# Cross-attention of a perceiver block with 32x32 tiles: VectorE block transposes in place of TensorE transposes

## What is computed

```python
Q = split_heads(layernorm(x) @ Wq + bq)          # 16 heads of 8 channels
K = split_heads(ctx_1024 @ Wk + bk)              # ctx_1024: (128 batches, 257 keys, 128)
V = split_heads(ctx_1024 @ Wv + bv)
energy = einsum('bhqd,bhkd->bhqk', Q, K) / sqrt(8)
energy = where(mask[:, None] == 0, -1e9, energy) # mask: (128, 32, 257)
out = einsum('bhqk,bhkd->bhqd', softmax(energy, -1), V)
x = x + out_as_128_channels @ Wo + bo
```

## Time and profile before

| what | value |
|---|---|
| median of 3 runs | 923.76 us |
| the profiled execution, its own time | 924.67 us |
| its span, first to last instruction | 922.9 us |
| mean granted TensorE clock | 0.961 of full speed |
| TensorE matmul busy | 833.8 us (90%) |
| TensorE weight load busy | 683.1 us (74%) |
| VectorE busy | 647.6 us (70%) |
| ScalarE busy | 583.9 us (63%) |
| GpSimd busy | 339.3 us (37%) |

### The profile page before, as it was taken

The page is one execution under the profiler, slowest core; times in us unless marked ns, Lnnn a source line. Parts: engine busy times, 40 slices in busy tenths (PEclk is TensorE's granted clock), DMA queues, the critical chain, the costliest instruction groups (busy, mean ns, idle before and its releaser), DMA issues.

```text
span 922.9 us, 28505 instructions
## 1 busy us (share of the span) xinstructions
PE 833.8 (90%) x10081; PEld 683.1 (74%) x10081; DVE 647.6 (70%) x1514; ACT 583.9 (63%) x1851; POOL 339.3 (37%) x334
## 2 busy tenths in 40 slices
PE   4699999999999999999995769999979999999998
PEld 2367777777777777777774658888869898999997
DVE  5568888888888888878885668778774445366633
ACT  2567777677777767767772469999945444433342
POOL 1447543544534434435411956666732000000000
PEclk9989999999999999999998879999966999999999
DMA  7283222222222222222500000000000000000100
GB/s 184 38 165 114 81 75 71 80 74 74 76 73 78 68 81 75 72 76 76 144 2 2 1 1 4 3 0 0 3 1 1 1 1 1 1 12 12 46 11 11
DMA packets 73163, 43.61 MB, mean 47 GB/s; under 512 B 8593, under 2 KB 72594, under 8 KB 73106
## 3 DMA queue, kind: packets, MB, share of 16 engines
q1 hardware_dynamic: 71808, 42.45, 16.9%
q10 hardware_dynamic: 1298, 0.40, 0.2%
HBM read 40.67 MB, written 2.16 MB: 46 GB/s over the span
## 4 chain that ended last, share of the span: by engine, by line
PE 58%; DVE 15%; ACT 13%; issue 8%; POOL 2%; DVEq 1%; ACTq 1%; DMA 1%; POOLq 0%
PE energy L397 30%; PE bank L400 17%; DVE STAT L1289 11%; PE bank L397 11%; ACT KS L518 4%; ACT KB L642 2%; ACT PR L526 2%; ACT xn L603 1%; ACT VB L631 1%; DVEq L1289 1%; POOL SX L783 1%; ACT xt L609 1%; POOL TQ L775 1%; DMA brow<-in_L_xattn_bo 1%; ACT SO L624 1%
## 5 line engine op out<-in xcount | busy, mean ns | idle before, releaser
L526 ACT ACTIVATE PR<-energy,STAT 128x256 f32<-128x256 f32 x512 | 237.0, 488 | 121.1 <-DVE STAT L1289 121.1
L1301 DVE COPY PT<-bank 128x512 f32<-128x512 f32 x256 | 170.2, 686 | 34.6 <-PE bank L400 33.3
L1289 DVE TENSOR_REDUCE STAT<-energy 128x512 f32 (+1 forms) x256 | 159.0, 685 | 46.4 <-PE energy L397 46.4
L400 PEld LDWEIGHTS bank<-ident,PR 128*128 128x128 f32 x1024 | 114.5, 142 | 75.1 <-issue 61.3
L400 PE MATMUL bank<-ident,PR 128*128 128x128 f32 x1024 | 149.4, 279 | 20.8 <-ACT KS L518 18.2
L397 PE MATMUL energy<-w_s,TQ 128*128 128x128 f32 x1024 | 124.9, 276 | 0.0
L397 PEld LDWEIGHTS energy<-w_s,TQ 128*128 128x128 f32 x1024 | 121.9, 192 | 3.2
L526 ACT ACTIVATION_READ_ACCUMULATOR PR<-energy,STAT (+1 forms) x512 | 112.4, 220 | 0.0
L709 POOL TENSOR_TENSOR QB<-QT,headmask 128x512 f32<-128x512 f32 x32 | 33.3, 1041 | 174.8 <-PE energy L397 156.4
L1529 DVE SCALAR_TENSOR_TENSOR X<-energy,GATE,X 128x128 f32<-128x128 f32 (+1 forms) x160 | 45.0, 344 | 71.8 <-PE energy L397 71.8
L716 POOL TENSOR_SCALAR MZ<-MK 128x512 bf16<-128x512 int32 x64 | 94.2, 1489 | 0.0
(11 more groups left out here) (205 smaller groups left out, 1503.5 us busy)
## 6 DMA issues: line engine op xcount, KB each, us to landing
CX<-in_ctx SPq DMA_DIRECT2D x128, 128.0 KB, 2.2
MK<-in_mask_BxSxS_ik SPq DMA_DIRECT2D x128, 128.0 KB
X<-in_x SPq DMA_DIRECT2D x4, 512.0 KB, 7.4
VLT<-v_last SPq DMA_DIRECT2D x4, 512.0 KB, 9.4
out<-X SPq DMA_DIRECT2D x8, 256.0 KB, 2.3
w_s<-in_L_ffn_W SPq DMA_DIRECT2D x1, 1024.0 KB, 7.6
xt<-in_ctx ACTq DMA_DIRECT2D x1, 64.0 KB, 4.0
ident<-const_ident ACTq DMA_DIRECT2D x1, 64.0 KB
```

Of the source, the lines that this page charges most:

```text
L400: return nc.tensor.transpose(o, i, ident[0:n, 0:n])
L526: nc.scalar.activation(PR[:, b, g, :], EB[:, g, e * KEYS:(e + 1) * KEYS], ACT.Exp, bias=STAT[:, bass.ds(t, 1), b, 1, g:g + 1].rearrange("p ...
L1289: V.tensor_reduce(STAT[:, bass.ds(t, 1), b:b + 2, 1, g:g + 1].rearrange("p a b g -> p (a b g)"), EB[:, g, :].rearrange("p (e k) -> p e k", ...
L1301: V.tensor_copy(PT[:, c // 2, 2 * half:2 * half + 2, :].rearrange("p g k -> p (g k)"), psum[1 if c % 2 else 7]).then_inc(ev_t, 1)
```

## The change

The loop goes over tiles of four batches in place of pairs. The rows of the energies become (batch of the tile, query), a head at a time: energies(t, s) fills the four banks for 8 of the 16 heads (s = 0, 1), each product a 32x32 tile of the array (32 rows of a group's channels in, 32 queries of one batch out), with 16 products for the mask and 32 for the energies. The probabilities of a head and batch are then transposed by VectorE in 32x32 blocks, SBUF to SBUF (turn: 8 instructions a tile, each 128x512), and attend() sums over 8 blocks of 32 keys with 128 products of 32x32 tiles. values() makes the values in blocks of 32 keys, 32 products of 128x32. TensorE's turns and VectorE's copies of them go. The copies out of PSUM of the context, the keys and the values are two banks wide and all on ScalarE; the result is copied by VectorE (evac_out). The banks 0, 1, 6, 7 are one tensor AUX that in turn holds the context and values, the keys, and the result of attend. Context and mask have two buffers of four batches in place of four of two. last_energies moves from the end into tile 3. The merge reads STAT where it lies. w1_s and w2_s share memory with the cross-attention's buffers, and their load waits for its last result. On GpSimd the addition of BROW to X moves behind tile 3, and a tile's mask is one instruction in place of two. Tiles 0 to 3, 30 and 31 are written out; 4 to 29 run in a hardware loop with two tiles in its body. pe_go is a semaphore that TensorE raises and nobody waits for.

The added code, with the removed lines mostly left out (they are the functions of the same names above):

```diff
-    out["same_query"] = (c[:, None] % SQ == c[None, :] % SQ).astype(one)
+    out["same_query"] = (c[:, None] % SQ == np.arange(SQ)[None, :]).astype(one)
...
-banks01 = [ctx.enter_context(nc.psum_tensor(f"bank{i}", [P, 512], F32)) for i in range(2)]
+AUX = ctx.enter_context(nc.psum_tensor("aux", [P, 4, 512], F32))
+psum = [AUX[:, 0, :], AUX[:, 1, :]] + [EB[:, k, :] for k in range(NG)] + [AUX[:, 2, :], AUX[:, 3, :]]
-query = sb("query", [P, P])
+query = sb("query", [P, SQ])
-w1_s = sb("w1_s", [P, E, F])
-w2_s = sb("w2_s", [P, E, FC, P])
-STAT = sb("STAT", [P, NT, BT, 2, NG])
+STAT = sb("STAT", [P, NT, 2, NH])
-CX = sbc("CX", [P, 4, 2, KC, P])
-VT = sbc("VT", [P, 4, 2 * KEYS])
+CX = sbc("CX", [P, 2, BT, KC, P])
+VT = sbc("VT", [P, 2, KBL, P])
-PR = sbc("PR", [P, BT, NG, KEYS])
-PT = sbc("PT", [P, 2, NG, KEYS])
+PR = sbc("PR", [P, 2, NG, 2, KEYS])
+PT = sbc("PT", [P, NH, KBL, SQ])
+w1_s = sb("w1_s", [P, E, F])
+w2_s = sb("w2_s", [P, E, FC, P])
...
+def tile_range(eng, tile):
+    for t in range(4):
+        tile(t, t % 2)
+    with eng.Fori(2, NT // 2 - 1) as i:
+        for h in range(2):
+            tile(2 * i + h, h)
+    for t in range(NT - 2, NT):
+        tile(t, t % 2)
+def static(t):
+    return isinstance(t, int)
...
+    def load_tile(t, i, h, first):
         if not first:
...
+            sp.wait_ge(pe_l, t - 1)
+        for b in range(BT):
+            sp.dma_start(CX[:, h, b, :, :], ctx_in[bass.ds(BT * t + b, 1), 0:KEYS, :]
+                         .rearrange("a (j p) c -> p (a j) c", p=P)).then_inc(ld_ctx[h], 16)
         if not first:
...
+            sp.wait_ge(pool_m, t - 1)
+        for b in range(BT):
+            sp.dma_start(MK[:, h, b, :], mask[bass.ds(BT * t + b, 1), :, 0:KEYS]
+                         .broadcast_to([4, SQ, KEYS])).then_inc(ld_mask[h], 16)
+    for t in range(2):
+        load_tile(t, 0, t, True)
...
+    with sp.Fori(1, NT // 2) as i:
+        for h in range(2):
+            load_tile(2 * i + h, i, h, False)
+    sp.wait_ge(ev_o, NT)
     sp.dma_start(w1_s[:, :, :], W1.rearrange("e c f -> c e f")).then_inc(ld_ffn, 16)
...
+    def evac_ctx(t, h):
+        act.wait_ge(pe_l, t + 1)
+        wait_reuse(act, pe_v, t - 1)
+        nc.scalar.activation(CT[:, h, :, :].rearrange("p b k -> p (b k)"),
+                             AUX[:, 0:2, :].rearrange("p a k -> p (a k)"), ACT.Copy).then_inc(ev_l, 1)
+    def evac_k(t, h):
+        act.wait_ge(pe_k, t + 1)
+        wait_reuse(act, pe_s, 2 * t - 2)
+        nc.scalar.activation(KS[:, h, :, :].rearrange("p b k -> p (b k)"),
+                             AUX[:, 2:4, :].rearrange("p a k -> p (a k)"), ACT.Identity,
+                             bias=bias[:, 1:2]).then_inc(ev_k, 1)
+    def evac_values(t, h):
+        act.wait_ge(pe_v, t + 1)
+        wait_reuse(act, pe_o, t - 1)
+        nc.scalar.activation(VT[:, h, :, :].rearrange("p k c -> p (k c)"),
+                             AUX[:, 0:2, :].rearrange("p a k -> p (a k)"), ACT.Copy).then_inc(ev_w, 1)
+    def exponents(t, s, g):
+        act.wait_ge(dve_min, 4 * (2 * t + s) + (g + 1))
+        if not (static(t) and t < 1):
+            act.wait_ge(ev_t, 4 * (2 * t + s) + (g - 7))
+        for h in range(2):
+            n = 4 * g + 2 * s + h
+            nc.scalar.activation(PR[:, s, g, h, :], EB[:, g, h * KEYS:(h + 1) * KEYS], ACT.Exp,
+                                 bias=STAT[:, bass.ds(t, 1), 1, n:n + 1].rearrange("p a n -> p (a n)"),
                                  scale=-1.0,
...
+                                 accum_out=STAT[:, bass.ds(t, 1), 0, n:n + 1]
+                                 .rearrange("p a n -> p (a n)")).then_inc(act_exp, 1)
+    def tile(t, h):
+        if not (static(t) and (t == 0 or t + 1 >= NT)):
+            evac_k(t + 1, 1 - h)
+        if not (static(t) and t == 0):
+            evac_values(t, h)
+        for g in range(NG):
+            exponents(t, 0, g)
+        if not (static(t) and t + 2 >= NT):
+            evac_ctx(t + 2, h)
+        for g in range(NG):
+            exponents(t, 1, g)
     nc.scalar.activation(warm[:, :], warm[:, :], ACT.Exp)
     evac_ctx(0, 0)
     evac_k(0, 0)
...
+    evac_values(0, 0)
+    evac_ctx(1, 1)
+    evac_k(1, 1)
     act.wait_ge(vl_ok, 1)
     act.dma_start(v_last, VL[:, :]).then_inc(st_vl, 16)
...
+    tile_range(act, tile)
+    act.wait_ge(m_diff, 2)
+    nc.scalar.activation(DIFF[:, :, :, :], DIFF[:, :, :, :], ACT.Exp).then_inc(m_exp, 1)
+    def ctx_transpose(t, i, h):
+        pe.wait_ge(ld_ctx[h], 16 * BT * i + 16 * BT)
+        if static(t) and t < 3:
+            wait_reuse(pe, ev_w, min(t, 1))
+            wait_reuse(pe, ev_l, t)
+        else:
+            pe.wait_ge(ev_o, t - 2)
+        for b in range(BT):
             for j in range(KC):
...
+                col = ((b % 2) * KC + j) * P
+                last = tr(AUX[:, b // 2, col:col + P], CX[:, h, b, j, :])
         last.then_inc(pe_l, 1)
...
+    def keys(t, h):
+        pe.wait_ge(ev_l, t + 1)
+        if static(t) and t < 3:
+            wait_reuse(pe, ev_k, t)
+        else:
+            pe.wait_ge(ev_o, t - 2)
+        for a in range(2):
+            last = mm(AUX[:, 2 + a, :], wk_s[:, :],
+                      CT[:, h, 2 * a:2 * a + 2, :].rearrange("p b k -> p (b k)"))
+        last.then_inc(pe_k, 1)
+    def values(t, h):
+        pe.wait_ge(ev_l, t + 1 if static(t) and (t == 0 or t + 1 >= NT) else t + 2)
+        if static(t) and t + 1 >= NT:
+            pe.wait_ge(ev_o, t - 1)
+        for k in range(KBL):
+            for b in range(BT):
+                last = mm(AUX[32 * b:32 * b + 32, k // 4, (k % 4) * P:(k % 4 + 1) * P],
+                          CT[:, h, b, 32 * k:32 * k + 32], wv_s[:, :])
         last.then_inc(pe_v, 1)
...
+    def energies(t, s, h):
+        pe.wait_ge(pool_m, t + 1)
+        pe.wait_ge(ev_k, t + 1)
+        pe.wait_ge(pool_q, t + 1)
+        wait_reuse(pe, act_exp, 8 * (2 * t + s))
+        pe.sem_inc(pe_go, 1)
+        for b in range(BT):
             for g in range(NG):
                 rows = slice(32 * g, 32 * g + 32)
...
+                mm(EB[32 * b:32 * b + 32, g, :].rearrange("p (a k) -> p a k", a=2), SEL_Q[rows, :],
+                   MZ[rows, h, b:b + 1, :].broadcast_to([32, 2, KEYS]), stop=False)
+        for a in range(2):
+            for b in range(BT):
+                for g in range(NG):
+                    rows = slice(32 * g, 32 * g + 32)
+                    last = mm(EB[32 * b:32 * b + 32, g, a * KEYS:(a + 1) * KEYS],
+                              QB[rows, h, b, 2 * s + a, :], KS[rows, h, b, :], start=False)
         last.then_inc(pe_s, 1)
...
+    def attend(t, h):
+        pe.wait_ge(ev_w, min(t + 2, NT) if static(t) else t + 2)
+        pe.wait_ge(ev_k, min(t + 3, NT) if static(t) else t + 3)
+        pe.wait_ge(ev_t, 8 * t + 8)
+        pe.sem_inc(pe_go, 1)
+        for k in range(KBL):
+            for b in range(BT):
+                rows = slice(32 * b, 32 * b + 32)
                 for g in range(NG):
...
+                    last = mm(AUX[32 * g:32 * g + 32, b, 0:P], VT[rows, h, k, 32 * g:32 * g + 32],
+                              PT[rows, 4 * g:4 * g + 4, k, :], start=(k == 0), stop=(k == KBL - 1))
+        last.then_inc(pe_o, 1)
     def last_energies():
         pe.wait_ge(klb_ok, 1)
...
         for t in range(NT):
             for b in range(BT):
                 n = t * BT + b
...
+                last = mm(AUX[32 * b:32 * b + 32, 2, 16 * t:16 * t + 16], QT[:, n * SQ:(n + 1) * SQ],
                           KLB[:, n, :])
         last.then_inc(pe_el, 1)
...
+    def tile(t, h):
+        energies(t, 0, h)
+        if not (static(t) and t == 0):
+            attend(t - 1, 1 - h)
+        if not (static(t) and t + 2 >= NT):
+            ctx_transpose(t + 2, t // 2 + 1 if static(t) else (t - h) // 2 + 1, h)
+        if static(t) and t == 3:
+            last_energies()
+        energies(t, 1, h)
+        if static(t) and t == 3:
+            pe.wait_ge(el_ok, 1)
+        if not (static(t) and t + 2 >= NT):
+            keys(t + 2, h)
+        if not (static(t) and t + 1 >= NT):
+            values(t + 1, 1 - h)
     pe.wait_ge(n0_qt, NT // 4)
     pe.wait_ge(brow_sp, 1)
     pe.wait_ge(sel_ok, 1)
     pe.wait_ge(ld_wx, N_X)
...
+    ctx_transpose(0, 0, 0)
     pe.wait_ge(dve_clt, 1)
...
+    mm(psum[4][:, 0:P], CLT, wv_s[:, :]).then_inc(pe_vl, 1)
+    mm(psum[5][:, 0:P], wk_s[:, :], CLT).then_inc(pe_kl, 1)
     keys(0, 0)
     values(0, 0)
...
+    ctx_transpose(1, 0, 1)
+    keys(1, 1)
     pe.wait_ge(vl_ok, 1)
     pe.wait_ge(klt_ok, 1)
...
+    tile_range(pe, tile)
+    attend(NT - 1, 1)
+    def key_minimum(t, s, g):
         if g == 0:
...
+            dve.wait_ge(pe_s, 2 * t + (s + 1))
+        n = 4 * g + 2 * s
+        V.tensor_reduce(STAT[:, bass.ds(t, 1), 1, n:n + 2].rearrange("p a n -> p (a n)"),
+                        EB[:, g, :].rearrange("p (h k) -> p h k", h=2), AX_X, ALU.min).then_inc(dve_min, 1)
+    def evac_out(t, h):
+        dve.wait_ge(pe_o, t + 1)
```

(35 more changed lines are left out.)

317 lines of the change are left out of this document (44 added, 273 removed).

## The result

The kernel after takes 1170.36 us (median of 4 runs, 1163.81 to 1171.13), the kernel before 924.08 us in the same comparison (923.61 to 925.91): a ratio of 1.264, with a 95% interval of 1.261 to 1.268. The forecast was 1015 us with a range up to 1045. The direction was right; of the size, +91 us were forecast and +246 measured, 2.7 times as much. The profiled run took 1163.81 us, a span of 1162.0, which is 239 us over the 922.9 of the span before.

A forecast was written before the change was run, and what follows sets the result against it. TensorE and an equally long ring of energies, minima and exponents were taken to bound the kernel. Start +16, written-out tiles +10, end -2 and refetched loop code +67 summed to +91 on 923.76: 1015 us, range 912 to 1045.

The forecast's parts named there:

- q8's count, over 130: Instruction queue's packets: near 60 if every block comes once, over 130 if the loop is fetched in each of 13 passes.
- v_last's store: Start: stored at 51, delaying VLT and tile 2's context; energies(0, 1) at 67, tile 1 at 73.5 against 57.3, +16 us.
- rival (b): VectorE's transposes handle each word twice, 1.38 us each, VectorE needs 16.7 a tile: +75, 1023 us; chance 0.08.
- The end: After the last exponents: coefficients 11 us later instead of 20, last_energies costing 7 in tile 3: -2; weights' load hidden.
- the second: fetched again: Cross-attention loop's 1968 TensorE instructions don't stay and are fetched every pass: 13 x (33.2 - 28.04) = +67 us; forecast's chance 0.58.
- A tile of new code: Tile whose TensorE code must be fetched: attend waits for blocks and ends at 7.0, energies(t, 1) at 9.1, tile 15.6 us.
- The jump: TensorE loop's jump back every two tiles: a fetch of 3.3 us, of which 2.0 is not hidden by the last exponents.
- The time of a block: TensorE code run once comes in blocks of 256 instructions at about 3.3 us each, no more than one block ahead.
- rival (a): Loop body stays in the engine and the ring decides: 13.35 us a tile, -17 in the loop, 931 us; chance 0.28.
- +10: Written-out tiles 1, 2, 3, 30 and 31 wait for code: 5 x (15.6 - 13.57) us.
- floor of 6.45: Ring from energies through minima and exponents to the next energies, without the KS copy: 6.45 us, twice that 12.9 a tile.
- Rival (c): 32x32 couples cost 25 ns each in a long run, attend ends at 8.6, tile 17.7: +96, 1044 us; chance 0.04.

The follow-up runs named there:

- a_unroll: Kernel after with TensorE's tiles 4 to 29 written out instead of looped, all other engines keeping their loops: 1115.7 us.
- e1_slot0: Kernel after with the head of TensorE's loop on the border of a 256-instruction block, without the hint: 1120.21 us.
- b_keys6: Kernel after without the values products of key blocks 6 and 7, loop body 1740 instructions: 1116.33 us.
- b_narrow: Kernel after with all instructions kept, but attend's products of the second half of the key blocks given one column instead of 128: 1154.25 us.
- experiment 4: Kernel after with the back-edge hint on TensorE's loop over tiles 4 to 29, body 1997 instructions: 985.93 us.

## Why the prediction was right or wrong

**Right.** Of two cases it took refetching, and q8's count, over 130, decided for it. v_last's store at 48.5 (forecast 51), energies(0, 1) at 68.7 (67), tile 1 at 76.4 (73.5). The transposes, whose price no row had:

```profile
L1275 DVE STREAM_TRANSPOSE PT<-PR 128x512 f32<-128x512 f32 x256 | 165.9, 687 | 9.4 <-ACT PR L534 6.6
```

687 ns where 690 was taken; rival (b) is out. ScalarE's wide copies took 1.03 to 1.15 us (1.14 taken). The end too, by the timeline (last transpose, first coefficients):

```profile
736.62 0.71 DVE L1275 STREAM_TRANSPOSE PT<-PR 128x512 f32<-128x512 f32 x1 [0.20 <-ACT PR L534]
...
747.99 0.87 POOL L763 TENSOR_TENSOR COEF<-DIFF,TOTAL 128x128 f32<-128x128 f32 x2
```

11.4 us lie between them, 11 were forecast, and the weights' load is hidden.

**Wrong: "the second: fetched again ... each tile 15.6 and at the jump back a fetch of which 2.0 is not hidden".** The mechanism came, fetching and its gaps. This term, +67, measured +201; both of its prices were too small, and a_unroll parts them:
- *A tile of new code: 15.6 forecast, 19.8 measured.* 26 x 4.2 = 109 of the 134 us. The forecast had energies(t, 1) start at 9.1 and a ring of 6.45 behind; in a_unroll these are 12.0 and 7.8 on the mean. In the tile shown there attend ends 9.4 us after the tile's start, forecast 7.0: it waits twice, 1.06 and 2.11 us, and the 128 couples of a block take 1.90 us, not 1.27. The transposes behind it take 1.94 us where 1.3 was taken.
- *The jump: 2.0 forecast, 3.9 measured* (43.5 less two of 19.8). 13 x 1.9 = 25 us. The body was counted as under eight blocks; ten were fetched in each pass.

The time of a block was too small too, 3.3 us from the bursts of the earlier trace rows, but no one number takes its place. In tiles 4 to 29 the instruction queue brought a packet each 4.4 us in the kernel after (128 in 565.4 us), 4.5 and 4.6 in e1_slot0 and b_keys6 (115 in 522.8 and 532.8), and 5.1 in a_unroll (101 in 514.6). My reading is that a block is not asked for while TensorE waits one ahead, so that the waits of the tile and those for code add up in part. No run here shows it.

**Wrong: the clock.** No term had it. The granted clock of the loop was 0.79, and pieces run at the lower of two levels behind many of the gaps. TensorE's busy time in tiles 4 to 29 is 75 us over that of the same couples with the hint. How much of it would have been waiting for code at full clock stays open: no run changes the clock alone, and b_narrow gave back as waits 8 of the 14 us of busy time that it saved.

**Wrong: the reason given for refetching.** Size alone did not decide (experiment 4). Had the loop carried the hint, the forecast's own likeliest case would have failed, and rival (a) would have been the story, though at 986 us and not at its 931: a kept tile costs up to 1.0 us more than (a) had, and the tiles that run once cost more than +10.

**Wrong: rival (a)'s 13.35 us.** A kept tile is 14.27 to 14.39. Attend takes 3.56 us for 256 couples, 13.9 ns each, where 9.9 from the earlier trace rows was taken; the first ring is 7.65, 0.75 over its 6.9. b_narrow shows that the columns count: 80 couples with one column take 0.92 us, 11.5 ns each, where 80 with 128 columns take 1.34. Energies in 80 couples delay the minima to 1.92 us after their start where the earlier trace rows have 1.47, which the floor of 6.45 left out, and the second ring is 6.74. The Trainium skill (TensorE: Matmul & The Clock Gate, "Wait — 56ns, not 53.3ns?") has a floor of about 25 ns from start to start; 13.9 ns on 32x32 tiles contradicts it, as the earlier trace rows did.

**Rival (c) is out** by the same 13.9 ns, where it needs 25.

**Slips in the sums.** Only the first enters the forecast's +91. With 80 couples left at 5.95 attend would have ended at 6.75, not 7.0, so the tile was 15.3 by its own terms. The array's part of attend is 256 x 34 / 4 = 2.2 us by the source that is named, not 1.7. Rival (b) is 26 x 2.7, not 2.9, so 1018; rival (c)'s tile adds up to 17.3, not 17.7, so 1032.

## What to carry to other kernels

Count a loop body's instructions beside the blocks that an engine keeps: here 7 blocks were kept without a hint, and a tight body of 8 or 9 was fetched again in each pass, 9 or 10 blocks at 4.4 to 4.6 us. Look at the instruction queue's packets first. If there are more than the program has blocks, hint the loop's closing branch, or use fewer and wider products, before anything else is tuned; and what runs once runs cold, so write few tiles out. A change that replaces large instructions by many small ones is paid in code as much as in array time.

## What the runs showed that I had not expected

- One hint on one loop took 184 us off (1170.36 to 985.93), and the body of 1997 instructions then stayed.
- A loop that isn't kept is slower than the same work written out: 1164 to 1171 against 1115.7 us.
- A heavy load slows code: blocks came 7.9 and 6.8 us apart while VLT's broadcast held 64% of the DMA engines.
- Without a hint, a loop's pass fetched one block more than its body touches by my reading of the compiled code (12 x 10 for 9, 12 x 9 for 8).
